# Turning the second half's input and the feed-forward weights by DMA instead of by TensorE, in a one-core decoder block

## The reference

```
x = LN(x + hyena(x))                       # first sub-layer
x = LN(x + ssm_attention(ctx, ctx, x))     # 32 heads of 8 batch rows
x = LN(x + ffn(x, w1, w2))                 # w1 2048x512, w2 512x2048

hyena:  xn = LN(x)*gamma + beta
        up = xn @ W_in.T + b_in            # 512 -> 1536 channels
        x0, x1, v = short_conv3(up)        # three taps along the time axis
        y = (long_conv(v*x1) + ...) * x0
        return y @ W_out.T
ffn:    weights: rms = rsqrt(mean(w*w)); clip(round(w*rms), -1, 1)/rms
        inputs:  rounded to 8 bits by row; gelu between the two products
```

## Time and profile before

| | |
|---|---|
| time, median of 3 runs | 1064.82 us (1059.51 to 1065.6) |
| the profiled execution | 1063.69 us |
| its span | 1061.9 us |
| mean granted TensorE clock | 0.989 of 2.4 GHz |
| TensorE products / weight loads busy | 1006.2 us (95%) / 602.9 us |
| VectorE / ScalarE / GpSimd busy | 799.3 / 599.9 / 552.7 us |
| DMA moved | 144.65 MB, mean 136 GB/s |
| hyena block, half 0 slots and setup | 0 to 182.3 us |
| output stage of half 0 | 182.3 to 246.2 us |
| slots of half 1 | 246.2 to 389.2 us |
| output stage of half 1, and end of the block | 389.2 to 459.9 us |
| heads block | 459.9 us to the end |

### The profile page before, as it was taken

One profiled execution on the slowest core, in us unless ns is written; L12 is line 12 of the kernel. 1 busy time (PEld: TensorE's weight loads), 2 busy tenths in 40 slices (PEclk: granted clock), 3 DMA queues, 4 the chain that ended last, 5 costly groups with the idle time before them and its releaser, 6 DMA issues.

```text
span 1061.9 us, 14827 instructions
## 1 busy us (share of the span) xinstructions
PE 1006.2 (95%) x4679; PEld 602.9 (57%) x4679; DVE 799.3 (75%) x1509; ACT 599.9 (56%) x728; POOL 552.7 (52%) x886
## 2 busy tenths in 40 slices
PE   3899999999999999978999999999999999999985
PEld 2455545544445555456666666666666666666641
DVE  7967975786475567657888888888888888888862
ACT  5655544112566558114666666767576767676664
POOL 5320310221000004269787887878787878787861
PEclk9999999999999999989999999999999999999998
DMA  9323655456475777441444544444444444444334
GB/s 322 61 60 120 203 152 163 145 165 194 162 227 189 241 259 255 141 143 51 105 98 113 105 113 108 115 106 117 104 117 105 109 114 101 122 99 114 76 64 91
DMA packets 178220, 144.65 MB, mean 136 GB/s; under 512 B 99988, under 2 KB 132792, under 8 KB 176120
## 3 DMA queue, kind: packets, MB, share of 16 engines
q1 hardware_dynamic: 178168, 144.00, 49.3%
HBM read 89.29 MB, written 33.70 MB: 116 GB/s over the span
## 4 chain that ended last, share of the span: by engine, by line
PE 50%; DVE 2%; POOL 1%; ACT 1%; DMA 1%; issue 1%; POOLq 0%; DVEq 0%; ACTq 0%
PE conv_bank L1398 28%; PE hq_bank L1421 9%; PE ff_bank L1442 5%; PE back_bank L1442 5%; PE back_bank L1412 1%; PE back_bank L1381 1%; PE ctx_bank L1369 1%; DMA hq_t<-hq_int 0%; POOL sum L1742 0%; DVE z L1607 0%; DVE g_max L1674 0%; POOL sum L1744 0%; ACT g L1546 0%; DMA xq_t<-xq_int 0%; ACT hq_f L1507 0%
## 5 line engine op out<-in xcount | busy, mean ns | idle before, releaser
L1742 POOL TENSOR_TENSOR sum<-z 128x640 f32<-128x640 f32 x128 | 198.2, 1549 | 11.6 <-DVE z L1619 9.6
L837 DVE SCALAR_TENSOR_TENSOR conv_all<-u,taps,conv_all 128x1024 f32<-128x1024 f32 x92 | 122.4, 1331 | 93.2 <-ACT conv_all L708 91.4
L1398 PE MATMUL conv_bank<-block_diag 128*128 128x288 f32 x628 | 167.8, 411 | 1.8 <-DVE z L1619 1.8
L1398 PE MATMUL conv_bank<-kv,block_diag 128*128 128x288 f32 x640 | 168.6, 406 | 0.9 <-DVE z L1619 0.8
L1398 PEld LDWEIGHTS conv_bank<-kv,block_diag 128*128 128x128 f32 x640 | 117.8, 190 | 31.6 <-DVE z L1619 1.8
L1398 PEld LDWEIGHTS conv_bank<-block_diag 128*128 128x128 f32 x628 | 117.3, 193 | 32.4 <-DVE z L1619 2.2
L1421 PE MATMUL hq_bank<-x_lo,hq_t 128*128 128x512 f16 x512 | 122.2, 382 | 4.7 <-DMA hq_t<-hq_int 4.7
L1674 DVE TENSOR_REDUCE g_max<-g 128x1 f32<-128x512 f32 x128 | 85.8, 673 | 41.5 <-ACT g L1546 41.5
L700 ACT ACTIVATE u<-slot_bank,bias,unscale 128x1024 f32<-128x1024 f32 x46 | 55.4, 1204 | 108.9 <-PE slot_bank L509 88.6
L1744 POOL TENSOR_TENSOR sum<-sum 128x320 f32<-128x320 f32 x128 | 111.3, 869 | 10.0
L1607 DVE TENSOR_TENSOR z<-conv_bank,qx 128x512 f32<-128x512 f32 x128 | 88.0, 687 | 34.2 <-PE conv_bank L1398 24.6
(11 more groups left out here) (181 smaller groups left out, 1676.2 us busy)
## 6 DMA issues: line engine op xcount, KB each, us to landing
x_quad<-in_w SPq DMA_DIRECT2D x10, 1024.0 KB, 8.3
v_scratch<-conv_all SPq DMA_DIRECT2D x16, 512.0 KB, 3.5
c_scratch<-v_tok SPq DMA_DIRECT2D x8, 1024.0 KB, 5.3
y<-c_scratch SPq DMA_DIRECT2D x8, 1024.0 KB, 4.9
res<-in_x SPq DMA_DIRECT2D x32, 256.0 KB, 2.9
x_scratch<-res SPq DMA_DIRECT2D x32, 256.0 KB, 3.1
block_diag<-in_ctx SPq DMA_DIRECT2D x32, 256.0 KB, 3.7
block_diag<-ssm_scratch SPq DMA_DIRECT2D x32, 256.0 KB, 3.7
```

The source lines that it names most:

```text
L837: ins = nc.vector.scalar_tensor_tensor(out=acc, in0=(u_first[kind] if n < 3 else u)[:, t0 + tap:t0 + tap + T // 2, :].rearrange("p t b -> ...
L1398: last = nc.tensor.matmul(view(conv_bank[tb % 2][:, hh, :], 0, (ROW64, T // 2), (1, PAIRS)), toep[:, head.buf, (tb - sb_) * P:(tb - sb_ + ...
L1742: nc.gpsimd.tensor_tensor(sum2[:, :, :], z[:, b, :, 0:half], z[:, b, :, half:2 * half], ALU.add).then_inc(sum2_done, 1)
```

## The change

For quads of half 1: ScalarE casts the normalized quad, in token order, to half precision (`make_hi`, one instruction of 2048 columns), VectorE subtracts (`make_lo`, one of 2048), and SyncE turns each of the two tiles with one DMA transpose straight into `x_hi` / `x_lo`, which are now laid out quad by quad. The halves lie in `conv[X1]`, `conv[V]`, `v_tok`, `conv[X0]`. For the weights: ScalarE packs the low 16 bits into a dense half-precision tile (`pack_part`, one instruction of 2048 columns), SyncE turns it with one DMA transpose into `w1_t` or `w2_t`. Half 0 is turned on TensorE as before. Slots 0 and 1 of half 1 wait for the turned halves; the block's end waits for all turned parts; reloads of `x_quad` wait for `lo_made` instead of for the TensorE transposes.

```diff
-        PART_AT = {1 + i: i for i in range(2 * PARTS)}
+        TURN_PART_AT = {2 + i: i for i in range(2 * PARTS)}
...
-        QUAD_AT = {1: 0, 4: 1, 9: 2, 13: 3}
+        HI_AT = {20: 0, 23: 1}
+        LO_AT = {22: 0}
+        LATE_LO_AT = {2: 1, 9: 2, 12: 3}
+        TURN_X_AT = {0: 0, 4: 1, 10: 2, 13: 3}
...
+                def turn_halves(q):
+                    if q == 0:
+                        sp.wait_ge(slot_full, NSLOT)
+                    for low, (made, x) in enumerate(((hi_made, x_hi), (lo_made, x_lo))):
+                        sp.wait_ge(made, q + 1)
+                        sp.dma_start_transpose(view(x[:, q, :, :], 0, (P, DC * QUAD), (1, P)), token_half(q, low)).then_inc(halves_turned[q], 16)
...
+                def turn_part(i):
+
+                    if i == 0:
+                        sp.wait_ge(slot_full, HALF * NSLOT)
+                    sp.wait_ge(packed, i + 1)
+                    if i < PARTS:
+                        out = view(w["w1_t"], i * DC * 512, (P, FC), (1, P))
+                    else:
+                        out = view(w["w2_t"], (i - PARTS) * P, (D, FC), (1, P))
+                    sp.dma_start_transpose(out, part_int[i]).then_inc(part_done, 16)
...
                         store_res(R)
+                        if hf + 1 < HALF and t in TURN_X_AT:
+                            turn_halves(TURN_X_AT[t])
                         if hf + 1 < HALF and t in LOAD_QUAD_AT:
                             load_quad(NQ * (hf + 1) + LOAD_QUAD_AT[t])
                         if hf + 1 == HALF and t == 0:
                             load_part(2 * PARTS - 1)
+                        if hf + 1 == HALF and t in TURN_PART_AT:
+                            turn_part(TURN_PART_AT[t])
+                sp.wait_ge(part_done, 2 * PARTS * 16)
...
-                        elif hf > 0 and s < 2 and j < 2:
-                            pe.wait_ge(made, DC * (NQ * hf + 2 * (s + 1)))
+                        elif hf > 0 and s < 2 and j == 0:
+                            for q in group:
+                                pe.wait_ge(halves_turned[2 * pr + q], 2 * 16)
...
-                        if hf + 1 == HALF and t in PART_AT:
-                            turn_part(PART_AT[t])
...
-                        if hf + 1 < HALF and t in QUAD_AT:
-                            turn_quad(NQ * (hf + 1) + QUAD_AT[t])
...
+                def make_hi(q):
+
+                    act.wait_ge(x_normed, q + 1)
+                    if q == 0:
+                        act.wait_ge(vx_done, 2 * DC)
+                    elif q == 1:
+                        act.wait_ge(v_stored, 2 * 16 * DC)
+                    elif q == 2:
+                        act.wait_ge(c_stored, 16 * DC)
+                    else:
+                        act.wait_ge(y_done, 4 * DC)
+                    src = quad_buf(NQ + q)[:, :, :].rearrange("p t d -> p (t d)")
+                    nc.scalar.copy(by_chunk(token_half(q, 0), QUAD * P, P), by_chunk(src, P, D)).then_inc(hi_made, 1)
...
+                def make_lo(q):
+                    dve.wait_ge(hi_made, q + 1)
+                    src = quad_buf(NQ + q)[:, :, :].rearrange("p t d -> p (t d)")
+                    hi, lo = (by_chunk(token_half(q, low), QUAD * P, P) for low in range(2))
+                    nc.vector.tensor_tensor(lo, by_chunk(src, P, D), hi, ALU.subtract).then_inc(lo_made, 1)
...
+                def pack_part(i):
+
+                    act.wait_ge(clipped, i + 1)
+                    if i == 0:
+                        act.wait_ge(c_stored, 16 * HALF * DC)
+                    else:
+                        act.wait_ge(packed, i)
```

More of the change, by code:

```diff
@@ L144, in hyena_block @@
         x_lo_done = sem("x_lo_done")
+        hi_made = sem("hi_made")
+        lo_made = sem("lo_made")
+        halves_turned = [sem(f"halves_turned{q}") for q in range(NQ)]
         u_zeroed = sem("u_zeroed")
@@ L204, in hyena_block @@
         rounded = sem("rounded")
-        part_turned = sem("part_turned")
+        packed = sem("packed")
         part_done = sem("part_done")
@@ L512, in slot, with convolve @@
                         last.then_inc(slot_full, 1)
[L514 removed]
+                def convolve(hf, cc, others=()):
                     first = chain_counts(hf, cc)
@@ L521, in convolve @@
                     for k in range(4):
-                        if quad is not None:
-                            pe.wait_ge(x_lo_done, DC * quad + k + 1)
-                        elif not others:
+                        if not others:
                             pe.wait_ge(ch_copied, first - 4 + k + 1)
@@ L587, in sum_matrix @@
                     nc.tensor.matmul(turn_bank[0][:, 0, 0:2], ones[:, :], total[:, :], start=True, stop=True).then_inc(summed, 1)
[L589 to L598, removed]
-                            fc = hh * FC // 2 + j
-                            last = nc.tensor.transpose(out[:, j * P:(j + 1) * P], low[:, fc * P:(fc + 1) * P], w["ident16"][:, :])
-                        last.then_inc(part_turned, 1)
                 def turn_first_ctx():
                     pe.wait_ge(early["ctx_reversed"], 1)
-                    pe.wait_ge(part_done, 2 * (2 * PARTS - 2) + 1)
+                    pe.wait_ge(ch_copied, 4 * HALF * DC)
                     for lb in range(LB):
@@ L639, in _ @@
                         for cc in pieces_after(s):
-                            others, quad = (), None
+                            others = ()
                             if hf == 0 and cc < DC - 1:
                                 others = [(w_lo_done, KINDS * (cc + 2))] + [(wout_done, DC)] * (cc == 0)
-                            elif hf > 0 and cc == 0:
-                                quad = NQ * (hf + 1) - 1
                             if hf == 0 and cc == 0:
@@ L650, in _ @@
                                 pe.wait_ge(mean_made, 1)
-                            convolve(hf, cc, others, quad)
+                            convolve(hf, cc, others)
                     for t in range(PARTIAL):
@@ L749, in round_part @@
                     nc.scalar.activation(part_raw[i], part_raw[i], ACT.Copy, scale=rms[:, m:m + 1], bias=LOW_HALF).then_inc(rounded, 1)
[L751 to L760 removed]
+                def pack_part(i):
[4 more added lines that the diff above has]
+                        act.wait_ge(packed, i)
+                    low = view(part_raw[i].bitcast(F16), 0, (2, F))
+                    if i < PARTS:
+                        out, src = view(part_int[i], 0, (DC * P, DC), (P, DC), (1, P)), view(low, 0, (2 * P, DC), (2 * D, DC), (2, P))
+                    else:
+                        out, src = part_int[i], low
+                    nc.scalar.activation(out, src, ACT.Copy, bias=-HALF_ONE).then_inc(packed, 1)
                 norm_first(0)
@@ L784, in _ @@
                             copy_conv(hf, cc)
+                        if hf == 0 and s in HI_AT:
+                            make_hi(HI_AT[s])
                         if hf + 1 == HALF and s in SQUARE_AT:
@@ L789, in _ @@
                     if hf + 1 < HALF:
-                        for q in range(NQ):
-                            split_hi(NQ * (hf + 1) + q)
+                        make_hi(2)
+                        make_hi(3)
                 for i in range(2 * PARTS):
@@ L1001, in _ @@
                             norm_quad(nxt + QUAD_NORM_AT[s])
+                        if more and s in LO_AT:
+                            make_lo(LO_AT[s])
                         if not more and s == TOTAL_AT:
@@ L1025, in _ @@
                             first_pairs()
-                        if more and t in QUAD_AT:
-                            split_lo(nxt + QUAD_AT[t])
+                        if more and t in LATE_LO_AT:
+                            make_lo(LATE_LO_AT[t])
                     res_norm(hf * T + T - 1)
```

51 lines of the change are left out of this document (17 added, 34 removed).

## The result

The kernel with the change takes 1085.97 us (median of 4, 1083.63 to 1089.5) against 1064.99 beside it: 1.0204 times as long, 95% interval 1.0167 to 1.0241. The forecast was 1087.9, slower. The profiled execution took 1083.63 us, its span 1081.8, against 1061.9 before: 19.9 us to find.

A forecast was written before the change was run, and what follows sets the result against it. TensorE was taken to pace the first output stage, with the store chain just behind, and the chain the second. 15.6 + 2.6 + 6.0 = 24.2 us on 1063.69 gave 1087.9 us, range 1070 to 1102.

The forecast's parts named there:

- What bounds the kernel: Output stages: TensorE sets the pace in the first, with the store chain just behind; the chain sets the second.
- the store chain: SyncE's queue: each residual load waits for the previous store's landing, the next store queues behind it; rounds of 3.56 us.
- Slot 1: Second half's slot 1 waits for the last transpose pair, queued behind store 13 in the first output stage: 15.6 us later.
- The clock: Behind TensorE's idle gap before slot 1, the granted clock is at its lower level of 1.2 GHz: 2.6 us.
- So nothing absorbs it: Slots behind slot 1 are TensorE-bound (139.4 of 143 us), so they shift by its full delay.
- Second output stage: Eight single transposes at time steps 2 to 9, each making a store chain round 0.75 us longer: 6.0 us.
- SyncE's own issue: SyncE's queue: 1.25 us to issue each transpose, inside the 3.1 us in which it waits for the store.
- 4.5 us for a single transpose, of 7 for the second of a pair: Sign of being right: landing times of the DMA transposes, 4.5 us single, 7 for a pair's second.
- The edits priced at zero: VectorE's subtractions and ScalarE's casts and packs sit beside other work and SyncE's wait for them costs nothing: zero.
- B: Rival, chance 0.2: transposes run like plain copies, 512 KB in 1.57 us; slot 1 is 6.0 late; 1072.3 us.
- D: Rival, chance 0.13: transposes disturb plain transfers by 0.8 us each, 3.55 us per transpose; 1100.7 us.
- C: Rival, chance 0.07: TensorE is the bound in both output stages, so the 18.0 us are won; 1045.7 us.

The follow-up runs named there:

- after_none: Changed kernel with each of its 16 transposes replaced by a copy of 64 of the 2048 columns, nothing turned: 1064.24 us, 0.9993 of the kernel before.
- after_none_res5: As after_none, with five places for the residual rows instead of four: 1043.7 us, 0.9798 of the kernel before.
- before_res5: The kernel before with five places for the residual rows instead of four: 1058.6 us, ratio 0.9957.
- x_only: Changed kernel with only the second half's x turned by DMA, the weights by TensorE as before: 1077.13 us, 1.0131 of the kernel before.
- after_plain: Changed kernel with each of its 16 transposes replaced by a plain, unturned copy of the same tile: 1069.53 us, 1.0034 of the kernel before.
- after_act: Changed kernel with all 16 transposes issued by ScalarE instead of SyncE: 1086.35 us, 1.0198 of the kernel before.
- after_res5: Changed kernel, whole transposes, with five places for the residual rows instead of four: 1071.03 us, 1.0058 of the kernel before.
- after: The kernel with the change itself, against the kernel before: 1085.97 us, ratio 1.0204.
- w_split_res5: Kernel before with only the weights turned by DMA, in transposes of 1024 columns behind stores 2 to 12, and five residual places: 1056.09 us, ratio 0.9928.
- w_split: Kernel before with only the weights turned by DMA, each part in two transposes of 1024 columns behind stores 2 to 14: 1071.84 us, ratio 1.0060.

## Why the prediction was right

Against the profiled execution the sum is 4.3 us too high (24.2 for 19.9). The median, 1085.97, lies nearer to the forecast's 1087.9 because the profiled execution was the fastest of the four. Term by term:

**What bounds the kernel: right.** In the second stage the store chain sets the pace, in the first it stands right behind TensorE. `after_none` and `after_none_res5` show it from both sides: without the transposes slot 1 comes no sooner with four places, and with five it comes 5.5 us sooner from the stage's first product (1.9 in `before_res5`).

**Slot 1: 15.6 predicted, 14.07 measured,** of which 0.5 is that the output stage began later in this execution. Store 13 left SyncE at 256.42, not 258.3. The rounds of the pairs are as worked out (3.56 + 3.5 = 7.06; stores 4 to 5 took 7.10, stores 10 to 11 took 6.76), but before, two other rounds of that stage were 6.3 us long (stores 3 to 4 and 6 to 7), and there the delay was partly taken up (3.93 and 4.31 after). I had credited only one slack of 0.9. From store 13 to slot 1 it was 9.0 us, for 8.6 predicted.

**The clock: 2.6 predicted, 2.74 measured**, on slot 1 itself. The price from the earlier trace rows fitted here, and in `x_only` (2.84) and `after_none` (2.75); in `after_plain` it was 1.95, behind a gap of 7.15 us, so it isn't the same wherever a gap stands. In `after_none` the gap was 4.41 us.

**"So nothing absorbs it": wrong, by 2.8 us.** The sentence rested on TensorE's busy share. That stage had a stall of 2.14 us, which a late start removes: 97% busy still leaves 3.6 us of idle time, and it can belong to something which a shift cures.

**Second output stage: 6.0 predicted, 6.67 measured.** Rounds of 4.62 us instead of 4.3. By the prediction's own rule the mis-sized term is the transpose's engine time, 3.10 us instead of 2.75 (4.62 is 1.10 more than an ordinary round of before, 3.52): a transpose of twice the size took 2.25 times the time of the earlier trace rows, where it ran alone. Eight rounds of before took 30.06 us with one of 5.42 among them, so the growth was 6.9 and not 8.5 us.

**SyncE's own issue, "1.25 us for each", "inside the 3.1 us in which it waits for the store": wrong.** It is 2.8 to 3.9 us in the second stage, and in seven of eight rounds the load leaves as soon as the issue ends, so it is this issue and not the store's landing that the load waits for. That the forecast held without this term can be luck in part: a round of SyncE's issues alone (store, transpose, load) comes to 4.4 us, close to what the engines' time gives, and full engines may be what stretches the issue. `after_act` took the issues off SyncE and won nothing, which speaks for the engines; what sets the 4.62 us, if one of the two does it alone, stays open. The landings of "4.5 us for a single transpose, of 7 for the second of a pair" failed too: 5.2 to 5.8 for the single ones of the second stage, 4.4 and 5.0 for the second of the last two pairs, which are issued 3.2 and 3.4 us after the first.

**The edits priced at zero** (casts, packs, the wait for them) cost nothing that the traces show: TensorE's gaps are released by DMA or by additions.

**Rivals.** B's price of plain copies is what `after_plain` has: slot 1 is 5.8 us late from the stage's first product, for 6.0 worked out, and the whole 3.9 us slower, for 8.6, since the clock cost 2.0 and the stall went. D's disturbance of 0.8 us isn't there in full (the median landing of a load went from 2.9 to 3.2), but a transpose's 3.10 us lie between the forecast's 2.75 and D's 3.55, and the 3.48 of `after_res5` is nearly D's. C needs another kernel: one without the chain and without the transposes' engine time.

## What to carry to other kernels

Before work is moved from a full engine to DMA, find the round that sets the pace and take its engine away in thought: here TensorE was busy 97% and its transposes were worth nothing until the landing of a store was out of the round. A transfer put into a latency-bound round costs little while it fits the round's gap (a plain copy 0.2 us, half a transpose 0.3 us a round here, for a gap of 2.0) and its excess beyond (a whole transpose, 3.10 us, made a round 1.1 longer); so price it by how long it holds the DMA engines and by how long its issue holds the queue, split it to fit the gap, and place the last piece well ahead of the stage's end. The cheap change was one more buffer.

## What the runs showed of the hardware

- A DMA transpose of 128x2048 half-precision values holds all engines for an estimated 3.10 us (`after`, from 1.01 x 4.62 - 1.57; 3.48 in `after_res5`) where a plain copy of the same 512 KB takes 1.45 (`after_plain`). The Trainium skill (Advanced Engine Details and Errata, X-Bar Transpose) has them as fast as regular DMAs; the runs disagree by a factor of 2.1, and 512 KB in 3.10 us is 169 GB/s.
- The packets say why they may be slow. The change adds 33,278 packets to 178,220, of which `after_plain` needs 2,302 for the same bytes; the packets under 512 bytes grow from 100,245 to 133,269 between these two: 2,064 for each transpose, 254 bytes in each. That small packets are the cause is argued, not shown.
- Two transposes of 1024 columns cost the engines about what one of 2048 does: in `w_split_res5`, 1.05 x 35.08 us less ten rounds of 1.57 leaves 1.51 us for each of the 14 in that stretch, 3.02 for two, where a whole one took 3.10 (`after`) and 3.48 (`after_res5`). Splitting moves the time; that it saves some isn't shown.
- The time in which SyncE issues a transpose grows with its size: 1.25 us for 1024 columns alone, 1.47 in `w_split`; for 2048 columns 2.2 to 3.4 us in the first stage of the change and 2.8 to 3.9 in the second, with the engines full. A plain copy of the same bytes takes 0.5.
